# Edge sums in a graph network kernel: block of nodes and further blocks kept per tile of 128 edges instead of per unit of four tiles

## The reference

```python
m_in = jnp.concatenate([h[src], edge_attr], axis=1)
m = jax.nn.relu(m_in @ W1.T + b1) @ W2.T + b2
agg = jax.ops.segment_sum(m, dst, num_segments=h.shape[0])
```

## Time and profile before

| | |
|---|---|
| median of 3 runs | 501.38 us (500.28 to 502.05) |
| the profiled execution | 502.33 us, its span 500.5 us |
| PE busy | 469.4 us (94%) |
| PE loading weights | 316.4 us (63%) |
| DVE busy | 296.0 us (59%) |
| ACT busy | 205.4 us (41%) |
| POOL busy | 105.5 us (21%) |
| granted clock of PE, mean | 0.987 |

### The profile page before, as it was taken

How to read it: one execution, slowest core, us unless ns; L and a number is a source line. 1 busy time by engine, 2 the same in 40 slices (tenths; PEclk the granted TensorE clock), 3 DMA queues, 4 the chain that set the end, 5 groups by cost and what they waited for, 6 DMA issues and landing times.

```text
span 500.5 us, 6858 instructions
## 1 busy us (share of the span) xinstructions
PE 469.4 (94%) x2310; PEld 316.4 (63%) x2310; DVE 296.0 (59%) x576; ACT 205.4 (41%) x368; POOL 105.5 (21%) x116
## 2 busy tenths in 40 slices
PE   7889987999979899899999999997899999999995
PEld 2334345666646566876756775674566688788884
DVE  5887797799778889565103579866123114542323
ACT  1788873456345443374126122674222004242000
POOL 0000287568766650000000240000000060000000
PEclk9999998899999999999999999999899999999998
DMA  8979678688878871999978799669987550200011
GB/s 252 428 270 411 208 209 272 192 265 258 278 246 269 269 239 45 412 341 379 372 302 296 317 326 359 241 289 369 381 339 283 204 169 1 85 1 1 22 43 42
DMA packets 29639, 121.21 MB, mean 242 GB/s; under 512 B 4330, under 2 KB 7354, under 8 KB 25246
## 3 DMA queue, kind: packets, MB, share of 16 engines
q1 hardware_dynamic: 17950, 92.33, 48.7%
q0 software_dynamic: 7856, 24.91, 16.1%
q10 hardware_dynamic: 3792, 3.43, 2.2%
HBM read 113.85 MB, written 6.82 MB: 241 GB/s over the span
## 4 chain that ended last, share of the span: by engine, by line
PE 66%; DMA 14%; DVE 12%; issue 4%; DVEq 2%; another core or an unknown queue 1%; ACT 0%; SPq 0%
PE ps L1446 13%; DMA basis<-in_basis 13%; PE ps L1501 12%; PE ps L1288 10%; PE ps L1539 9%; PE ps L1324 6%; DVE x L1000 3%; PE ps L1484 3%; PE ps L1372 3%; PE ps L1376 3%; PE ps L1373 2%; DVE rlo L1007 2%; PE ps L1254 1%; DVE X L935 1%
## 5 line engine op out<-in xcount | busy, mean ns | idle before, releaser
L1324 PE MATMUL ps<-xT_lo,xT_hi 128*128 128x512 f32 x237 | 62.6, 407 | 7.9 <-DVE x L1000 6.9
L1288 PE MATMUL ps<-basis,sel 128*32 128x512 f32 x496 | 59.0, 605 | 4.9 <-DMA basis<-in_basis 4.9
L609 POOL DMA_INDIRECT X<-u_rows,esrc x40 | 44.3, 1107 | 77.6 <-DMA u_rows<-X 56.8
L618 POOL DMA_DIRECT2D X<-w_layer x32 | 16.8, 653 | 206.8 <-DMA w_layer<-ev 206.8
L1324 PEld LDWEIGHTS ps<-xT_lo,xT_hi 128*128 128x128 f32 x237 | 42.9, 191 | 25.7 <-DVE x L1000 10.1
L609 POOL DMA_INDIRECT x_sb<-u_rows,esrc x39 | 43.3, 1110 | 18.5 <-issue 9.5
L1539 PE MATMUL ps<-Xr,CT_r 128*128 128x512 f32 x200 | 47.0, 389 | 0.0
L1539 PEld LDWEIGHTS ps<-Xr,CT_r 128*128 128x128 f32 x200 | 37.5, 188 | 7.8
L697 ACT ACTIVATE rhi<-x 128x512 fp32r<-128x512 f32 x60 | 35.5, 630 | 16.9 <-DVE x L1000 13.2
L1159 DVE SCALAR_TENSOR_TENSOR Xr<-ps,gate,Xr 128x512 fp32r<-128x512 f32 x20 | 14.9, 750 | 45.7 <-ACT Xr L796 45.7
L1007 DVE SCALAR_TENSOR_TENSOR rlo<-x,rhi 128x512 fp32r<-128x512 f32 x60 | 39.5, 687 | 0.0
(11 more groups left out here) (232 smaller groups left out, 810.9 us busy)
## 6 DMA issues: line engine op xcount, KB each, us to landing
basis<-in_basis SPq DMA_DIRECT2D x29, 2048.0 KB
X<-in_eaT SPq DMA_DIRECT2D x20, 256.0 KB
basis<-in_basis SPq DMA_DIRECT2D x8, 512.0 KB
X<-w_layer POOLq DMA_DIRECT2D x32, 128.0 KB, 3.0
w_layer<-ev SPq DMA_DIRECT2D x13, 256.0 KB, 10.6
X<-in_WhhT SPq DMA_DIRECT2D x3, 1024.0 KB, 14.9
basis_apart<-in_basis SPq DMA_DIRECT2D x1, 2048.0 KB, 19.0
X<-in_WihT SPq DMA_DIRECT2D x2, 1024.0 KB, 10.1
```

Of the source, the lines that this page charges most:

```text
L609: nc.gpsimd.indirect_dma_start(gat[e % GATHERS], None, t["u"][:, :], bass.IndirectOffsetOnAxis(ap=esrc[:, e:e + 1], axis=0)).then_inc(gat_ ...
L1288: mm = pe.matmul(bank[32 * g:32 * g + 32], sel[:, layer, s], held[:, g, s2], start=(s == 0), stop=(s == 3), tile_position=(0, 32 * g))
L1324: mm = pe.matmul(ps[:, EA_BANKS[s]], part[:, u % 2, s * P:(s + 1) * P], w, start=(i == 0), stop=(i == 2))
```

## The change

A unit's word now holds four first blocks, one per tile, and whether any of its tiles has a further block (`unit_windows`). Each tile has a word of its own with its first block, the number of further blocks and the count of further passes so far (`tile_windows`); it is loaded only in units that have some. DVE subtracts the tile's first block times 128 from the destinations once, ahead of the stage (a matmul that spreads the first blocks over the partitions, and one operation), so the base one-hots compare with the fixed numbers 0 to 127. PE's base sums take each tile's bank from its own register. For further blocks there is a branch and a loop per tile: one 128x128 one-hot, and the matmuls of that tile alone.

```diff
--- before.py
+++ after.py
...
 FILLED = -(-E // P)
-BEFORE = NT + UNITS + 1
 EA_BANKS = (5, 7, 6, 6)
...
         sprow = sb("sprow", [1, 2, ET])
-        uspan = sb("uspan", [1, 3, UNITS])
-        winf = sb("winf", [1, UNITS + 1])
-        winp = sb("winp", [1, 2, UNITS])
-        wins = sb("wins", [1, UNITS], I32)
+        extra_of = x1[0:1, 4, 0:ET]
+        extras_upto = x1[0:1, 4, ET:2 * ET + 1]
+        packed = x1[0:1, 4, 2 * ET + 8:3 * ET + 8]
+        wins = x1[0:1, 4, 256:256 + ET].bitcast(I32)
+        more = x1[0:1, 4, 384:384 + UNITS]
+        firsts = [x1[0:1, 4, 416 + h * 32:416 + h * 32 + UNITS] for h in range(2)]
+        unit_wins = x1[0:1, 4, 480:480 + UNITS].bitcast(I32)
         flagf = sb("flagf", [1, 2])
...
-        def windows(eng, tile):
-            v = eng.value_load(wins[0:1, tile:tile + 1], min_val=0, max_val=PACK * PACK * (NT + 1) * UNITS)
-            first = (v % PACK).with_bounds(min_val=0, max_val=NT - 1)
-            end = (v // PACK % PACK).with_bounds(min_val=1, max_val=NT)
-            return [first, end, v // (PACK * PACK)]
+        def unit_windows(eng, u):
+            v = eng.value_load(unit_wins[0:1, u:u + 1], min_val=0, max_val=PACK ** (UNIT + 1))
+            return v // PACK ** UNIT, [((v // PACK ** t if t else v) % PACK).with_bounds(min_val=0, max_val=NT - 1)
+                                       for t in range(filled(u))]
+        def tile_windows(eng, e):
+            v = eng.value_load(wins[0:1, e:e + 1], min_val=0, max_val=PACK * PACK * NT * ET)
+            return (v % PACK).with_bounds(min_val=0, max_val=NT - 1), (v // PACK % PACK).with_bounds(
+                min_val=0, max_val=NT - 1), v // (PACK * PACK)
...
             dve.nop().then_inc(hi_ready, UNIT)
-            dve.nop().then_inc(next_ready, BEFORE)
+            dve.nop().then_inc(next_ready, 1)
             dve.memset(epst[:], LN_EPS)
             dve.memset(sel[:], 0.0)
-            step(dve.memset(winf[:, 0:1], 0.0))
+            dve.memset(extras_upto[:, 0:1], 0.0)
             dve.memset(hot[:, :, P + SPAN:], 1.0)
...
                     dve.tensor_copy(sprow[:, 0:2], ps[0:1, 4, 0:2 * ET].rearrange("p (q t) -> p q t", q=2))
+                    nc.vector.scalar_tensor_tensor(out=dstf[:], in0=ps[:, 4, 272:272 + ET], scalar=-float(P),
+                                                   in1=dstf[:], op0=ALU.mult, op1=ALU.add)
                     step(dve.tensor_copy(att[:].rearrange("p g l r -> p (g l r)"), ps[:, 4, 256:256 + 4 * REL]))
...
-                    by_unit = sprow[:, 0:2].rearrange("p q (u s) -> p q u s", s=UNIT)
-                    dve.tensor_reduce(uspan[:, 0], by_unit[:, 0], AX.X, ALU.min)
-                    step(dve.tensor_reduce(uspan[:, 1], by_unit[:, 1], AX.X, ALU.max))
-                    step(nc.vector.scalar_tensor_tensor(out=uspan[:, 2], in0=uspan[:, 1], scalar=1.0,
-                                                        in1=uspan[:, 0], op0=ALU.add, op1=ALU.subtract))
-                    step(dve.tensor_tensor_scan(winf[:, 1:UNITS + 1], uspan[:, 2], uspan[:, 2], 0.0, ALU.add, ALU.bypass))
-                    dve.tensor_scalar(winp[:, 0], uspan[:, 1], 1.0, None, ALU.add)
-                    step(dve.tensor_tensor(winp[:, 1], winf[:, 0:UNITS], uspan[:, 0], ALU.subtract))
-                    step(dve.tensor_scalar(winp[:, 1], winp[:, 1], float(NT), float(PACK), ALU.add, ALU.mult))
-                    step(dve.tensor_tensor(winp[:, 1], winp[:, 1], winp[:, 0], ALU.add))
-                    step(dve.tensor_scalar(winp[:, 1], winp[:, 1], float(PACK), None, ALU.mult))
-                    dve.tensor_tensor(wins[:], winp[:, 1], uspan[:, 0], ALU.add).then_inc(wins_ready, 1)
+                    step(dve.tensor_tensor(extra_of, sprow[:, 1], sprow[:, 0], ALU.subtract))
+                    dve.tensor_reduce(more, extra_of.rearrange("p (u s) -> p u s", s=UNIT), AX.X, ALU.max)
+                    step(dve.tensor_tensor_scan(extras_upto[:, 1:], extra_of, extra_of, 0.0, ALU.add, ALU.bypass))
+                    step(nc.vector.scalar_tensor_tensor(out=packed, in0=extras_upto[:, 0:ET], scalar=float(PACK),
+                                                        in1=extra_of, op0=ALU.mult, op1=ALU.add))
+                    nc.vector.scalar_tensor_tensor(out=wins, in0=packed, scalar=float(PACK), in1=sprow[:, 0],
+                                                   op0=ALU.mult, op1=ALU.add)
+                    first_of = sprow[:, 0].rearrange("p (u s) -> p s u", s=UNIT)
+                    sofar = more
+                    for s in range(UNIT - 1, -1, -1):
+                        into = firsts[s % 2] if s else unit_wins
+                        last = nc.vector.scalar_tensor_tensor(out=into, in0=sofar, scalar=float(PACK), in1=first_of[:, s],
+                                                              op0=ALU.mult, op1=ALU.add)
+                        sofar = into
+                        if s:
+                            step(last)
+                    last.then_inc(wins_ready, 1)
                 if w == 2:
...
-            def one_hots(into, u, j):
-                nodes = iota[:, bass.ds(j * P, P)].rearrange("p (s n) -> p s n", s=1).broadcast_to([P, UNIT, P])
+            def one_hots(u):
+                nodes = iota[:, 0:P].rearrange("p (s n) -> p s n", s=1).broadcast_to([P, UNIT, P])
                 ends = dstf[:, u * UNIT:(u + 1) * UNIT].rearrange(
                     "p (s n) -> p s n", n=1).broadcast_to([P, UNIT, P])
-                return dve.tensor_tensor(into, nodes, ends, ALU.is_equal)
-            def unit(u, bounds):
-                first, end, before = bounds
+                dve.tensor_tensor(oh[:, u % 2], nodes, ends, ALU.is_equal).then_inc(oh_ready, 1)
+            def unit(u, extras_here):
                 dve.wait_ge(sums_done, u + 1)
-                one_hots(oh[:, u % 2], u, first).then_inc(oh_ready, 1)
+                one_hots(u)
                 split(u, (0,))
...
                 split(u, range(1, SPLITS))
-                ahead = windows(dve, (u + 1) % UNITS)
+                ahead, _ = unit_windows(dve, (u + 1) % UNITS)
                 if u == 6:
...
-                with dve.If(end > first + 1):
-                    with dve.Fori(first + 1, end) as j:
-                        dve.wait_ge(next_free, j + before + (UNITS - u + 1))
-                        one_hots(oh_next[:], u, j).then_inc(next_ready, 1)
+                with dve.If(extras_here > 0):
+                    for t in range(filled(u)):
+                        e = u * UNIT + t
+                        _, extra, before = tile_windows(dve, e)
+                        with dve.If(extra > 0):
+                            with dve.Fori(1, extra + 1) as d:
+                                dve.wait_ge(next_free, before + d + 1)
+                                dve.tensor_scalar(oh_next[:, t], iota[:, bass.ds(d * P, P)], dstf[:, e:e + 1], None,
+                                                  ALU.is_equal).then_inc(next_ready, 1)
                 if u < UNITS - 1:
...
             dve.wait_ge(wins_ready, 1)
-            bounds = windows(dve, 0)
+            extras_here, _ = unit_windows(dve, 0)
             for u in range(UNITS):
-                bounds = unit(u, bounds)
+                extras_here = unit(u, extras_here)
...
             pe.nop().then_inc(extra_free, GPACK + 1)
-            pe.nop().then_inc(next_free, BEFORE + 1)
+            pe.nop().then_inc(next_free, 2)
             pe.wait_ge(setup_ready, 1)
...
                                        start=True, stop=True)
+                    mm = pe.matmul(ps[:, 4, 272:272 + ET], span7[:, 0:1].broadcast_to([ET, P]), ident[0:ET, 0:ET],
+                                   start=True, stop=True)
                     mm.then_inc(span_row, 1)
...
-            def window_sums(picked, u, j):
-                into = ps[:, bass.ds(j, 1)].rearrange("p b n -> p (b n)")
-                for s in range(filled(u)):
-                    if s < SPLITS:
-                        pe.matmul(into, picked[:, s], rhi[:, u % 2, s], start=False, stop=True, skip_group_check=True)
-                        mm = pe.matmul(into, picked[:, s], rlo[:, u % 2, s], start=False, stop=True,
-                                       skip_group_check=True)
-                    else:
-                        mm = pe.matmul(into, picked[:, s].bitcast(F32), pre[:, s], start=False,
-                                       stop=True, skip_group_check=True)
-                return mm
-            def sums(u, span):
-                first, end, before = span
+            def tile_sums(window, picked, u, t):
+                into = ps[:, bass.ds(window, 1)].rearrange("p b n -> p (b n)")
+                if t == SPLITS:
+                    return pe.matmul(into, picked.bitcast(F32), pre[:, t], start=False, stop=True,
+                                     skip_group_check=True)
+                pe.matmul(into, picked, rhi[:, u % 2, t], start=False, stop=True, skip_group_check=True)
```

(22 more changed lines are left out.)

## The result

The changed kernel takes 514.83 us (median of 4 runs, 508.85 to 516.86) against 501.72 for the kernel before in the same series; the ratio is 1.022, with a 95% interval of 1.0142 to 1.0297. Ratios are taken of fast runs alone, here without the one of 516.86 us and with a fifth of 512.72. In a later series the unaltered pair gave 515.91 and 502.06. The change costs 13 to 14 us by the medians, 11 by the first ratio, whose interval goes from 7 to 15; the forecast was 513.0, or +11.6. The profiled execution of after is its fastest run, 508.85 us, with a mean granted clock of 0.984; the clocks of its other runs are 0.971 to 0.973. So this trace shows less of the clock's part than most runs hold.

The account below looks back on a forecast made before the run. The prediction took PE to bound the crossing units, with DVE level in plain ones. Net control 6.2, clock 5.1 and setup 0.3 gave +11.6 us, 513.0 against a median of 501.38; range 502 to 519.

Parts of the forecast that it names:

- What bounds: Edge sums: DVE and PE both set plain units' pace; PE sets the four crossing units, whose changes go straight to the end.
- The saved pass: Crossing units' second pass: 1.4 us saved in each of three with a fourth tile, 1.8 with a first tile, 6.0 altogether.
- The control: PE's sequencer in crossing units: 1.1 us per skipped tile, only 2.3 us covered; net of saved matmuls +6.2 us.
- The range's upper end, +8: Crossing units on PE: upper bound of the +6.2 us net term, with a fifth more for each control step.
- The rival that the control hides: Crossing units: register work done while the array runs, only the 6.0 us saving counts, 495.7 us; chance 0.13.
- DVE: Crossing units: DVE's control ends near 101.2, PE frees it at 101.8, so not quite the bound; first tile's unit ties.
- The clock: Gaps of about 3 us on PE in crossing units: clock falls behind three of four, 1.7 us each, +5.1 (0 to 10).
- Plain units: The 16 other units: new tile addresses lie under the previous tile's matmuls, 0, between -0.1 and +0.1 us a unit.
- Setup: Stage before the edge sums and w == 1: an added matmul and subtraction, +0.3 us on DVE's chain, bounds 0 and 0.5.

Follow-up runs that it names:

- static kernel: Changed kernel with the crossing tiles written into the program on PE and DVE, no run-time control: 497.57 us (0.9906) on chip A, 497.58 us (0.9894) on C.
- one-tile kernel: Changed kernel asking only the crossing tile at run time, the three others left out: 491.23 us (0.9993) on chip B, 504.36 us (1.0037) on C.
- static-PE kernel: Changed kernel with PE's further sums written out for these inputs, DVE's run-time control unaltered: 496.09 us, 1.0084 against the kernel before, chip B.
- second trace of after: Profile from a repeat of the changed kernel, unaltered, on chip A: 515.91 us against 502.06 for the kernel before, 1.0276.
- the zeros: Changed kernel with 14 matmuls of zeros ahead of the control in crossing units, control unaltered: 510.5 us, 1.0139 against the kernel before, chip A.
- static-DVE one: Changed kernel with DVE's further one-hots written out for these inputs, PE's run-time control unaltered: 507.39 us, 1.0298 against the kernel before, chip B.
- one-word kernel with static DVE: Changed kernel, PE deciding from one word per unit without loads per tile, DVE's further one-hots written out: 488.54 us, 0.9936 against before, chip B.
- one-word kernel on A: Changed kernel with one word per unit holding four first blocks and counts, no load per tile: 504.78 us, 1.0043 against the kernel before, chip A.

## Why the prediction was right

**What bounds.** Right. A longer unit on PE lengthens the whole: static control gives back 18.3 us at the end, and the crossing distances of the two traces on A differ by as much (43.9 against 25.6).

**The saved pass.** Forecast -6.0; the static kernel's crossing distances show -5.2, and its time -4.5 and -5.2 on two chips, setup included. For the fourth tiles the 1.4 each holds (1.44, 1.35, 1.40). The first tile's 1.8 holds for the closing matmul (4.58 to 2.81) but not for the distance (7.67 to 6.70, so 0.97). The other kernels with a cheap first tile have distances of 6.17 to 7.26 there; in the static one DVE idles 1.02 us ahead of its next add for something that the trace doesn't show. The forecast took it that a whole saving on PE arrives.

**The control.** The mechanism was right, its size a little small: +7.7 instead of +6.2 (2.0 + 1.5 + 2.1 + 2.1 by the closing matmul; 7.5 by the distances without the fall). The step that was short is the head of the control and its end. The first load stands 0.94 after the first matmul, not 0.74; the three skipped tiles take 3.3, as forecast, and 1.10 by the one-tile kernel; from the last load to the extra matmuls it is 154.26 - 152.8 = 1.5 where 1.4 was counted: 5.7, not 5.4. The two matmuls take 0.96 instead of 0.87. The range's upper end, +8, took it in. The rival that the control hides needs under 0.6 us a tile. With one tile asked it does hide but for 0.15 us (closing at 3.35 against the static 3.2). With no load for a tile a gap of 0.37 us is left, and the closing is 0.6 to 0.7 later than the static one. The Trainium skill, page "Advanced Engine Details and Errata", section Sequencer Loop, says that further instructions are read and queued while control is worked; the traces agree for the 2.3 us of the base sums (the first load stands at 149.5, they end at 151.05). They also show what ends the lead, a semaphore wait: in before the wait for rlo ends at 94.31 and the sums' address is worked at 94.4.

**DVE.** Right, and close: forecast 0.6 us behind PE, and the static-PE kernel shows 0.5. Its adds start 3.6 us after PE's first matmul, forecast 3.0; PE's closing was late by 0.4. Only for the unit of the first tile, where a tie was forecast, does DVE stand further behind, 0.9 us.

**The clock.** Forecast three falls and +5.1. The second trace of after has three, worth 5.7; filling the gaps brings 5.4 us, up to 6.4 with the cost of the zeros. The price of one, 1.7, holds nearly: the fall of the first trace took 1.6 us in the 12 matmuls behind it (4.58 - 2.98), two of the second 1.5 (10.47 against 10.55 - 1.6) and 1.3 (11.10 - 9.76); the third, low already in the extra matmuls, took about 2.7 (12.47 - 9.80). The number of three was a guess that came true: the first trace has one fall, worth 1.6 in all, the static-DVE one four. The time at the lower level in each run is the better witness: about 26 us in after against 10.

**Plain units and setup.** Plain units: 0, as forecast; undisturbed they keep 5.4 to 5.5 us, as the earlier trace rows. Setup: the first sums matmul is at 73.29 and was at 72.53, one unit ahead of the one in the earlier trace rows; kernels with the same setup have it between 72.51 and 73.55, so 0.3 can't be told from 1.

**The sum.** 7.7 in the crossing units, 5.4 of clock and 0.3 to 1 of setup make 13.4 to 14.1, against 13.1 and 13.9 measured by the medians. Put the other way: the control's 18.3 us are 12.6 in the crossing distances (38.2 less 25.6) and 5.4 to 5.7 of clock. The excess over the forecast's 11.6, 1.5 to 2.3 us, is the control's mis-sized term and up to 0.7 of setup. That the sum comes out so close is in part luck. It leaves out two things that neither forecast nor experiment explains, and in the traces they nearly cancel: plain distances shorter by 5.0 and 3.2 us for waits for rows that fell elsewhere, and a stretch behind the sums longer by 1.6 and 3.1.

## What to carry to other kernels

Where a finer decision saves array work, add up what the sequencer does per item asked, from loads to branches, and set it against the array work issued since the last semaphore wait; here 1.1 us per tile bought 0.5 us of matmuls per tile saved. Ask items only after a cheap test says which, from a word that is already in a register: without loads per tile the closing matmul came at 3.9 us instead of 6.7, though the whole kernel got no faster than before. And price an idle TensorE above its length: where three of four gaps of 3 us brought a fall, they cost about 1.4 us more each on average.

## What was not expected of the hardware

The kernel before takes 490.7 us on chip B and 502.1 and 502.8 on A and C, with the same program. In after's trace and those of A and C, DVE waits for gathered rows now here, now there; in those of B hardly at all: the plain distances are 84.1 to 85.2 us in sum there, 91 to 102 elsewhere, which is about what the chips differ by. Why, no run shows. The page of the one-word kernel with static DVE on B:

```profile
L1013 DVE TENSOR_TENSOR x<-ps,X 128x512 f32<-128x512 f32 x40 | 26.0, 682 | 4.5 <-PE ps L1340 2.1
...
L1013 DVE TENSOR_TENSOR x<-ps,x_sb 128x512 f32<-128x512 f32 x39 | 25.0, 681 | 1.2 <-DMA x_sb<-u_rows,esrc 1.0
```

Idle 5.7 us in the two groups, against 16.2 in the one-word kernel on A. Such waits also come with gaps on PE (3.40 us ahead of 92.25 in after, then 0.50 over 93 to 98), so they spend clock as well. And the fall behind a gap is not certain: behind 2.91 us at 132.18 it came, behind 3.21 at 154.26 and 3.24 at 181.95 it did not in the same execution, while the kernel with static DVE fell behind 3.20 at 150.68. A good part of a term like that lies in the draw of the execution, and one profile can't size it.
